# Unread products in TensorE's first pauses, weight loads placed by period, row turns in PSUM bank 0 and the output projection in bank 5

## What is computed

```python
x = x + attn(layernorm(x), w_qkv, w_out)            # 16 heads of 8, causal
x = x + xattn(layernorm(x), ctx, ctx, times, ...,   # 16 heads of 8, keys/values by bucket
              pad, bucket_ids, Wq, Wk_b, Wv_b, Wo, bo)
x = x + ffn(layernorm(x), ...)                      # 4-head attention over batches, then 8 experts
# bucket weights: K = key @ Wk_b[bucket], V = value @ Wv_b[bucket], 8 buckets
# experts are linear: (tokens @ w1[e] + b1[e]) @ w2[e] + b2[e]
```

## Time and profile before

| | |
|---|---|
| median of 3 runs | 389.6 us (388.9 to 390.59) |
| the profiled execution's own time | 389.38 us |
| its span in the trace | 387.6 us |
| busy: PE, DVE, ACT, POOL | 338.2, 271.8, 148.1, 100.5 us |
| mean granted TensorE clock | 0.968 |
| chain that ended last: share of PE, ACT, DVE | 73%, 9%, 6% |

### The profile page before, as it was taken

One profiled execution on the slowest core, in us unless ns is written; L12 is line 12 of the kernel. 1 busy time (PEld: TensorE's weight loads), 2 busy tenths in 40 slices (PEclk: granted clock), 3 DMA queues, 4 the chain that ended last, 5 costly groups with the idle time before them and its releaser, 6 DMA issues.

```text
span 387.6 us, 12234 instructions
## 1 busy us (share of the span) xinstructions
PE 338.2 (87%) x4813; PEld 227.2 (59%) x4813; DVE 271.8 (70%) x703; ACT 148.1 (38%) x398; POOL 100.5 (26%) x165
## 2 busy tenths in 40 slices
PE   3798898999999899999999998876899599699994
PEld 2444454666665464655555555663656346599993
DVE  5775787666667788878898986343455189448996
ACT  2123364556665354554546463432244412100000
POOL 1136443000011435453233423126000023301111
PEclk9999999999999999999999999996999999569999
DMA  8999533344722525125000000000000000000001
GB/s 223 339 244 299 133 90 107 118 131 140 215 88 96 128 76 138 49 84 111 2 3 3 2 2 3 3 0 3 2 2 3 2 0 1 2 2 13 22 23 54
DMA packets 29192, 28.63 MB, mean 74 GB/s; under 512 B 4312, under 2 KB 24808, under 8 KB 29008
## 3 DMA queue, kind: packets, MB, share of 16 engines
q1 hardware_dynamic: 26848, 24.24, 22.1%
q0 software_dynamic: 1280, 3.15, 3.1%
q10 hardware_dynamic: 1008, 0.46, 0.5%
HBM read 20.17 MB, written 7.67 MB: 72 GB/s over the span
## 4 chain that ended last, share of the span: by engine, by line
PE 73%; ACT 9%; DVE 6%; issue 5%; another core or an unknown queue 3%; DMA 2%; ACTq 1%; POOL 1%; POOLq 0%; DVEq 0%
PE ps L1067 9%; PE ps L1084 8%; PE ps L1029 7%; PE ps L1370 7%; PE ps L1039 3%; PE ps L1003 3%; PE ps L1114 3%; PE ps L1148 3%; PE ps L982 3%; ACT pT L804 3%; PE ps L995 2%; PE ps L1219 2%; ACT pT L920 2%; PE ps L1161 2%
## 5 line engine op out<-in xcount | busy, mean ns | idle before, releaser
L804 ACT ACTIVATE pT<-ps 128x512 f32<-128x512 f32 x128 | 70.4, 609 | 98.1 <-PE ps L1039 88.3
L407 DVE TENSOR_REDUCE m_pad<-ps 128x8 f32<-128x1024 f32 x32 | 39.2, 1224 | 35.0 <-PE ps L1067 35.0
L701 POOL TENSOR_TENSOR rstd<-veps,minus_half 128x1 f32<-128x1 f32 x32 | 19.1, 598 | 137.7 <-DVE veps L372 137.0
L383 DVE TENSOR_TENSOR p_sb<-qk_sb,heads 128x512 f32<-128x512 f32 x64 | 44.0, 687 | 1.8 <-DMA ident_bf<-c_ident_bf 1.4
L410 DVE TENSOR_REDUCE m_pad<-ps 128x8 f32<-128x1024 f32 x32 | 38.9, 1215 | 0.0
L1067 PE MATMUL ps<-p_sb,qk_sb 32*128 32x512 f32 x256 | 38.4, 671 | 0.0
L1084 PE MATMUL ps<-pT,p_sb 128*32 128x128 f32 x1024 | 36.8, 276 | 1.5 <-issue 1.5
L1029 PE MATMUL ps<-p_sb,qk_sb 32*128 32x512 f32 x256 | 38.0, 655 | 0.0
L765 POOL TENSOR_TENSOR rs<-ve,half 128x2 f32<-128x2 f32 x16 | 11.2, 698 | 99.2 <-DVE ve L610 99.2
L1039 PE MATMUL ps<-mT,negsel 32*128 32x128 f32 x512 | 34.6, 364 | 0.8 <-issue 0.7
L1370 PE MATMUL ps<-mexp,pT 128*128 128x128 f32 x256 | 34.4, 291 | 0.6 <-DVE pT L675 0.6
(11 more groups left out here) (176 smaller groups left out, 640.3 us busy)
## 6 DMA issues: line engine op xcount, KB each, us to landing
room<-mask_rows SPq DMA_DIRECT2D x32, 128.0 KB, 3.3
wkv_sb<-wkv SPq DMA_DIRECT2D x23, 128.0 KB
kv_sorted<-room SPq DMA_DIRECT2D x5, 512.0 KB, 4.8
ctx_sorted<-room SPq DMA_DIRECT2D x1, 1472.0 KB, 12.5
tk<-fside SPq DMA_DIRECT2D x1, 1024.0 KB, 9.5
mask_rows<-y1T SPq DMA_DIRECT2D x8, 128.0 KB, 2.7
out<-y SPq DMA_DIRECT2D x8, 128.0 KB, 1.8
x_sb<-x SPq DMA_DIRECT2D x1, 768.0 KB, 6.9
```

The costliest lines, as they stand in the source:

```text
L383: return dve.tensor_tensor(dst, rows.unsqueeze(1).broadcast_to([128, QUADS, S]), heads[:, 0, :].unsqueeze(2).broadcast_to([128, QUADS, S]) ...
L407: dve.tensor_reduce(m4[:, 0:2, 0:QUADS], ps[:, 0:2, :].rearrange("p g (j k) -> p g j k", j=QUADS), AX.X, ALU.max).then_inc(s["max_low"], 1)
L701: pool.tensor_tensor(rstd[:, :], veps[:, :], minus_half[:, :], ALU.pow)\
L804: act.activation(pT[:, t % 2, g, :, :], quad[4 + g], ACT.Exp).then_inc(s["exped"], 1)
```

## The change

Five edits that come together:

1. TensorE issues matmuls of a tile of ones with itself into bank 4, which nothing reads: 9 before it waits for the identity, 2 ahead of `project_qkv(1)`, 2 ahead of `project_qkv(2)` and 3 behind it. Each has 128 x 512 bf16 as its moving operand.
2. SP no longer issues all loads first. Times and pads wait for `pv_done` 2, cross weights come behind the first sorted group, each expert's two matrices wait for `pv_done` 15 + e, the small ones come in three parts between. `pad_masks` and `cross_masks` are one period later, and one mask load waits for the first gather instead of all stores of sorted keys and values.
3. The normalised rows are turned in bank 0, columns 128 to 255, not in bank 1. ACT copies them between `exp_group` 0 and 1, without waiting for `pv_done`; `turn_max` waits for that copy.
4. The output projection goes to bank 5, columns 384 to 511. `scores_by_query` and `turn_heads` then wait for ACT's copy `fT_copied`, not for `resid_done`; `scores_by_key`, `copy_qk` and `project_out` itself wait for `resid_done`.
5. TensorE does `project_qkv(p+3)` ahead of `project_out(p-3)`.

```diff
+            def expert_weights(e):
+
+                sp.wait_ge(s["pv_done"], 15 + e)
+                sp.dma_start(w1t_sb[:, e, :, :], w1t[e].rearrange("(c p) d -> p c d", p=128))\
+                  .then_inc(s["experts_in"], 16)
+                sp.dma_start(w2_sb[:, e, :, :], w2[e].rearrange("(c p) d -> p c d", p=128))\
+                  .then_inc(s["experts_in"], 16)
...
             bucket_weights(0)
             bucket_weights(1)
+            sp.wait_ge(s["pv_done"], 2)
+            times_and_pads()
...
-            for done in kvs_stored:
-                sp.wait_ge(done, 8 * SORT_GROUPS)
+            sp.wait_ge(kv_in[0], 32)
             masks_by_group(1)
+            expert_weights(0)
+            expert_weights(1)
             masks_to_rows(2)
+            small_weights(0)
             masks_by_group(2)
+            expert_weights(2)
+            small_weights(1)
+            expert_weights(3)
+            small_weights(2)
+            expert_weights(4)
...
-                dve.tensor_tensor(rows, rows, bank[2][:, 128:256], ALU.add).then_inc(s["resid_done"], 1)
+                dve.tensor_tensor(rows, rows, bank[5][:, 384:512], ALU.add).then_inc(s["resid_done"], 1)
...
-                if p == 3:
+                if p == 4:
                     pad_masks()
-                if 0 <= p - 3 < B:
-                    cross_masks(p - 3)
+                if 0 <= p - 4 < B:
+                    cross_masks(p - 4)
...
             def turn_xn(t):
                 act.wait_ge(s["xT_done"], t + 1)
-                if t >= 4:
-                    act.wait_ge(s["pv_done"], t - 3)
                 if t >= 1:
                     act.wait_ge(s["qkv_done"], t)
-                act.copy(xnT[:, :], bank[6 if t == 2 else 1][:, 256:384]).then_inc(s["xnT_copied"], 1)
+                act.copy(xnT[:, :], bank[6 if t == 2 else 0][:, 128:256]).then_inc(s["xnT_copied"], 1)
...
             def copy_qk(t):
                 act.wait_ge(s["qkv_done"], t + 1)
+                if t >= 6:
+                    act.wait_ge(s["resid_done"], t - 5)
...
                     exp_group(p, 0)
+                if live(p + 3) and p != -1:
+                    turn_xn(p + 3)
+                if live(p):
                     exp_group(p, 1)
...
+            def idle_products(n):
+
+                for _ in range(n):
+                    pe.matmul(quad[4], ones_bf[:, :], ones_bf[:, :].unsqueeze(1).broadcast_to([128, QUADS, S]),
+                              start=True, stop=True, skip_group_check=True)
+
+            pe.wait_ge(s["ones_ready"], 4)
+            idle_products(9)
             pe.wait_ge(s["ident_in"], 16)
...
             def turn_max(t):
                 pe.wait_ge(s["max_low"], t + 1)
                 pe.wait_ge(s["max_high"], t + 1)
+                pe.wait_ge(s["xnT_copied"], min(t + 3, T))
...
                 if t >= 1:
-                    pe.wait_ge(s["resid_done"], t)
+                    pe.wait_ge(s["fT_copied"], t)
                 pe.transpose(bank[2][:, 0:128], o_sb[:, t % 2, :], ident[:, :]).then_inc(s["fT_done"], 1)
...
+                if t >= 4:
+                    pe.wait_ge(s["resid_done"], t - 3)
                 pe.wait_ge(s["qk_copied"], min(t + 3, T))
...
                     if g == 2 and t >= 5:
-                        pe.wait_ge(s["resid_done"], t - 4)
+                        pe.wait_ge(s["fT_copied"], t - 4)
...
-                pe.matmul(bank[2][:, 128:256], ofT[:, :], w_out_sb[:, t // B, :], start=True, stop=True)\
+                pe.wait_ge(s["exped"], min(4 * t + 14, 4 * T))
+                if t >= 1:
+                    pe.wait_ge(s["resid_done"], t)
+                pe.matmul(bank[5][:, 384:512], ofT[:, :], w_out_sb[:, t // B, :], start=True, stop=True)\
                   .then_inc(s["proj_done"], 1)
...
+                if p == -2:
+                    idle_products(2)
+                if live(p + 3) and p != -1:
+                    project_qkv(p + 3)
                 if live(p - 3):
                     project_out(p - 3)
-                if live(p + 3) and p != -1:
-                    project_qkv(p + 3)
...
                 if p == -2:
+                    idle_products(2)
                     project_qkv(2)
+                    idle_products(3)
```

More of the change, by code:

```diff
@@ L271, in bucket_weights, with times_and_pads, cross_weights, small_weights @@
                       .then_inc(wkv_in[i % 2], 16)
+            def times_and_pads():
+                sp.dma_start(tk[:, :, :], fside.partition_broadcast(128)).then_inc(s["times_in"], 16)
+                sp.dma_start(tq[:, :], fsideT).then_inc(s["times_in"], 16)
+                sp.dma_start(pad_words[:, :, :], pad.partition_broadcast(128)).then_inc(s["times_in"], 16)
+                sp.dma_start(padT_words[:, :], padT).then_inc(s["times_in"], 16)
+            def cross_weights():
+                sp.dma_start(wq_sb[:, :], wq).then_inc(s["xw_in"], 16)
+                sp.dma_start(w_out_sb[:, 1, :], wo).then_inc(s["xw_in"], 16)
+                sp.dma_start(bo_rows[:, :], bo.partition_broadcast(128)).then_inc(s["xw_in"], 16)
+            def expert_weights(e):
[4 more added lines that the diff above has]
+                  .then_inc(s["experts_in"], 16)
+            small = [(inw_sb[:, :], inw), (inb_col[:, :], inb), (inb_rows[:, :], inb_v.partition_broadcast(128)),
+                     (ow_sb[:, :], ow), (ob_rows[:, :], ob.partition_broadcast(128))]
+            small += [(ln_rows[:, i, :], v.partition_broadcast(128)) for i, v in enumerate((g1, be1, g2, be2))]
+            small += [(b1t_sb[:, :, :], b1t.rearrange("(c p) e -> p c e", p=128)), (b2_sb[:, :], b2),
+                      (wg_sb[:, :], wg), (samepos[:, :], c_samepos), (rank[:, :, :], c_rank),
+                      (batchof[:, :], c_batchof), (pick_all[:, :], c_pick_expert[:, E, :]),
+                      (pick_expert[:, :, :], c_pick_expert[:, 0:E, :])]
+            nloads[0] = len(small)
+            def small_weights(part):
+                for dst, src in small[6 * part:6 * part + 6]:
+                    sp.dma_start(dst, src).then_inc(s["ffn_w_in"], 16)
             def masks_to_rows(i):
@@ L306, in _ @@
                     bucket_weights(i + 2)
-                if i == 1:
+                if i == 0:
+                    cross_weights()
+                if i == 2:
                     masks_to_rows(0)
-                if i == 2:
+                if i == 3:
                     masks_by_group(0)
             masks_to_rows(1)
-            for done in kvs_stored:
-                sp.wait_ge(done, 8 * SORT_GROUPS)
+            sp.wait_ge(kv_in[0], 32)
             masks_by_group(1)
+            expert_weights(0)
+            expert_weights(1)
             masks_to_rows(2)
+            small_weights(0)
             masks_by_group(2)
+            expert_weights(2)
[3 more added lines that the diff above has]
+            expert_weights(4)
             masks_to_rows(3)
             masks_by_group(3)
+            for e in range(5, E):
+                expert_weights(e)
             for i in range(B // 2):
@@ L875, in _ @@
                     turn_heads(p - 3)
-                if live(p + 3) and p != -1:
-                    turn_xn(p + 3)
                 if live(p + 1):
@@ L972, in turn_xn @@
                     pe.wait_ge(s["xnT_copied"], t)
-                pe.transpose(bank[6 if t == 2 else 1][:, 256:384], xn[:, :], ident[:, :]).then_inc(s["xT_done"], 1)
+                pe.transpose(bank[6 if t == 2 else 0][:, 128:256], xn[:, :], ident[:, :]).then_inc(s["xT_done"], 1)
             def turn_o(t):
@@ L1052, in scores_by_query @@
                     if g == 0 and t >= 1:
+                        pe.wait_ge(s["xnT_copied"], min(t + 2, T))
                         pe.wait_ge(s["mT_copied"], t)
-                    if g == 1:
-                        pe.wait_ge(s["xnT_copied"], min(t + 2, T))
-                        if t >= 3:
-                            pe.wait_ge(s["oT_copied"], t - 2)
+                    if g == 1 and t >= 3:
+                        pe.wait_ge(s["oT_copied"], t - 2)
                     if g == 3 and t >= 4:
```

24 lines of the change are left out of this document (2 added, 22 removed).

## The result

The changed kernel takes 380.64 us (median of 4 runs, 376.6 to 383.45), the kernel before 390.1 beside it (4 runs, 388.9 to 390.98): 9.5 us less by the medians; ratio 0.9683, 95% interval 0.9616 to 0.9749. The ratio goes by the two faster executions of the changed kernel (376.6 and 378.67 us, 12.4 us less), the median by all four, and the profile shows one of the two slower. The profiled execution took 382.61 us, 2.0 above its median, with a span of 380.8 and a mean granted clock of 0.952 (0.968 before).

The account below looks back on a forecast made before the run. TensorE was taken as the bound. Terms 2.8 + 0.9 + 6.6 + 0.4 = 10.7 us off the span of 387.6 gave 376.9, with the 1.8 around it 378.7; its own range 376 to 381.5, with rivals 373.5 to 385.

Parts of the forecast that it names:

- The start: At the start, the products of ones bring TensorE's clock to 2.4 GHz by about 12 us: 2.8 us less.
- rival (a): At the start, the clock rises late, by the second scores: 1.0 us instead of 2.8, 380.5 us; chance 0.17.
- The waits for `xnT`: In the early periods, ACT's new order takes out waits of `project_qkv` for `xnT`: 0.9 us less, ends 0.4 and 1.2.
- The order and bank 5: In 20 periods (3 to 5, 12 to 28), `project_qkv` fills TensorE's pause: 0.33 us each, 6.6 us less.
- The end: At the end of the kernel, `turn_heads` no longer waits for the residual: 0.4 us less.
- The loads: Loads issued later: direct effect 0 us; 4 us kept for the range in case full DMA engines cause early stops.
- Rival (b): In the early periods, the light DMA load also removes the stops, 4 us: 374.7 us; chance 0.15.
- Rival (e): In periods 15 to 22, stops follow the 16 expert loads, 1.2 us each: slower, 398 us; chance 0.04.
- (c): In cross periods, DVE or TensorE's sequencer takes over, the order gives 0.1 each: 4.6 us less gain, 383.3; chance 0.12.
- (d): Whole kernel: products do nothing for the clock and the order gives nothing either: 388 to 389 us; chance 0.04.

## Why the prediction was right, and where it was not

The forecast of 378.7 us held: 380.64, within its own range of 376 to 381.5, and 9.5 us saved (12.4 by the faster executions) of 10.7. That the sum held is in part luck. The order gave more than its term, the start less, and stops that no term stood for took some of it back; on the second chip, where these stops are absent, the same change saved 381.49 - 367.34 = 14.2 us, more than the 13.4 that the range reached to, and on the third 12.1.

**The start: 2.8 forecast, 1.4 to 1.7 measured, and not visible in the first pair.** The cost was right (4.02 us for the nine against 3.9, and covered). The step that was too large is "if the clock is at 2.4 GHz by about 12 us". It was there at 9.75 and gone at 14.40, since TensorE has nothing to do while DVE makes `xn` (2.64 us). Of the seven profiles with products on the second and third chip, six have tile 0's scores in the low clock, at least in part, and tile 1's at 1.14 in all; TensorE had stood 1.9 to 2.7 us ahead of tile 0's. In the seventh, the one with spread loads, it stood 1.0 us, tile 0's already take 1.14 at 12.39, and tile 2's 2.09: there the earlier rise was given back later. Scores that are fast from the second on are rival (a)'s course; the 1.4 to 1.7 lies between its 1.0 and the forecast's 2.8. On the first chip the stop behind 32 us covers it, so there I can't say what the start gave.

**The waits for `xnT`: 0.9.** In the ratio bank 0 alone gave nothing (0.9884 against 0.9885), but that can't tell 0.9 us. The profiles can. In periods 1 and 2, from the scores of tile 2 to those of tile 4, the kernel with bank 0 alone needs 11.56 us (5.59 + 5.97), and the kernel before and the one with the loads alone, both on the same chip, need 12.26 (6.13 twice): 0.7 us less. In its profile the stop of 0.91 us in period 3 takes this back.

**The order and bank 5: 6.6 forecast, 9.7 measured.** The mechanism was right. The size was held down by "DVE is about level with TensorE at this gain and caps it there". The same two cross periods (from the scores of tile 28 to those of tile 30) on the second chip, first of the kernel before and then of the changed one, show that it does not:

```profile
211.05:223.99 12.94, 12.25 (x229) 7.25 (x215) 11.19 (x28) 6.98 (x22) 4.68 (x11) 1.00 0.01 3
```

```profile
199.77:211.71 11.94, 11.94 (x231) 7.20 (x215) 10.96 (x28) 6.92 (x21) 4.78 (x12) 1.00 0.01 3
```

TensorE's idle time, 0.69 in two periods, is gone altogether (the other 0.31 of the gain was counted as busy), and DVE still has 0.98 to spare (1.75 before). A period gains 0.50 and not 0.33, near the top of the 0.3 to 0.55 that I had worked out "before what other engines allow". 17 periods (12 to 28) by 0.50 are 8.5; the changed kernel's 111.62 us against the 118.92 of the loads alone, with 1.2 us more of stop in periods 18 and 19, make about the same. Tile 2 to 7 needs 30.73 us against 32.66 with bank 0 alone, 1.9 less, but 0.9 of this is that kernel's stop in period 3, which leaves 1.0 for the order, as forecast. The experiment with bank 2 adds what the prediction did not say: the new order alone is worth nothing, since the pause moves behind the residual.

**The end: 0.4.** From tile 31 to the end of the span 147.6 us before, 146.6 after on the first chip, 148.0 and 145.8 on the second. The kernel with bank 0 alone has 147.0, and so has the changed kernel on the third chip, while the one with the order but bank 2, where `turn_heads` still waits for the residual, has 146.2. Both pairs show a gain larger than the term, but the wait that I named is not shown to be its cause, and the late low-clock stretch is in it.

**The loads: 0 forecast, 2.8 alone.** The failed step is "Direct effect: 0". I followed the waits in front of the loads and not what stands behind the wait that was exchanged: the first gather behind eight mask loads. On the first chip the kernel before has no such row, which is why it was not to be read there; what I could have asked is which of the two DMAs TensorE needs first. Inside the changed kernel the new placing gave nothing on the third chip (369.16 without it, 369.53 with it): the wait for the gather goes (1.5 us in period 13), and the stop in period 19 comes, 2.1. With the loads spread out the stop is gone.

**Rival (b), full DMA engines make the early stops.** The rows speak against it: from 30 to 40 us the share fell from 0.96 to 0.28, and the long stops of the first chip stayed and grew. On two other chips neither kernel has them, light load or heavy (0.97 in the kernel before on the second). Their cause stays open; in these runs they go with the first chip and not with this change.

**Rival (e), stops that follow the expert loads.** Stops of this kind exist, one or two in a run and with up to 2.1 us, not 16 times with 1.2. (The sign would have turned at 10.7 / 16 = 0.7 us each, not at 0.8.) The Trainium skill, Runtime: NRT & Kernel Launch, section "Instruction fetch mechanics", has each sequencer fetch its code by DMA in blocks, "mostly hidden". The rows of period 19 fit a fetch that is not hidden while the DMA engines are full. That full engines belong to it is borne out by the spread loads and by the profiles counted above, five of six against none of five. They are not enough by themselves: the kernel with bank 0 alone ran through 1.08 in period 18 without a stop, and the kernel before on the second chip through 0.97 from 30 to 40 us, a 16 KB block among its transfers. That it is the fetch and not another wait is only argued, by the place between equal matmuls; in the changed kernel on the second chip the block had landed (155.64) when its stop of 1.51 us began (155.71).

**Rivals (c) and (d).** (c), an engine that takes over in the cross periods, is refuted by the 5.97 us; (d), that neither products nor order do anything, by order and bank 5 (0.9624 against 0.9884) and by tile 1's scores at 1.14.

## What to carry to other kernels

Work moved into a pause gains nothing when the wait behind it ends no sooner than before (377.78 against 377.05 us): find both waits, and remove the two together. Before counting another engine as the cap, sum its idle time over the whole period and not in the places nearest to the edit. When DMAs are reordered, ask for each which one the busiest engine waits for next, and where the places of bulk loads can be chosen, try them spread out: TensorE can stop while the DMA engines are full though it waits for none of the data (7.92 us for a period of 5.87).

## What the runs showed of the hardware

- The same kernel takes 390.1 us on one chip and 381.5 to 381.7 on two others. The first has long stops of ACT, DVE and TensorE in the self periods, with small products a few at a time (4 to 6 in the changed kernel), 0.75 us apart, and no releaser. The others have none of these, but single stops of TensorE of 0.4 to 1.8 us.
- TensorE's matmuls were at the high clock at 9.75 us (0.45 for two) and at the low one at 13.41 (0.48 for one) after 2.64 us without work. At the third scores the clock fell in four kernels, behind two waits of 0.8 to 1.2 us for DVE, and in three others it did not behind the same two; the changed kernel is in both groups (1.91 on the first chip, 1.14 on the third). In period 13 it fell behind waits of 1.85 and 3.09 us (scores of 2.09), and not behind waits of 0.45 and 1.4.
- Nine products of 512 columns with nothing else running take 4.02 us at the start, 0.45 each; three of them at 17.66, with the clock high, take 0.81.
- Full DMA engines went with a stop of TensorE of 1.67 us in the middle of a group of matmuls (1.51 on the second chip), and with shorter or no stops in other profiles.
